# Narrow causal heads in two layers: compact q and k projections moved to their rows by DMA, four heads at a time in two slots of four banks, division after the last unit

## The reference, cut to what matters

```python
# layer 0
q, k, v = split(x @ w_attn.T + b_attn)             # 16 heads of width 16
scores = einsum('bhqd,bhkd->bhqk', q, k) * 0.25
probs = softmax(where(causal, scores, -inf))
ctx = einsum('bhqk,bhkd->bhqd', probs, v)
out = ctx @ w_proj.T + b_proj
# layer 6
A1 = causal_sdpa(q1, k1, v)                        # 16 heads, q and k of width 8, v of width 16
A2 = causal_sdpa(q2, k2, v)
diff = A1 - lam * A2
diff = (1 - lambda_init) * diff / sqrt(mean(diff * diff) + eps)   # the mean over each head's 16
out = diff @ Wproj
```

## Time and profile before

| | us |
|---|---|
| median of 3 runs | 2824.78 (2816.72 to 2827.63) |
| the profiled execution, its own time | 2828.42 |
| its span in the profile | 2826.4 |
| layer 0, from its first matmul to its last transposes | 15.24 to 182.99 |
| layer 6, from its first matmul to the end of its first output projections | 915.69 to 1236.25 |
| PE busy over the span | 2196.2 |

### The profile page before, as it was taken

One profiled execution on the slowest core, in us unless ns is written; L12 is line 12 of the kernel. 1 busy time (PEld: TensorE's weight loads), 2 busy tenths in 40 slices (PEclk: granted clock), 3 DMA queues, 4 the chain that ended last, 5 costly groups with the idle time before them and its releaser, 6 DMA issues.

```text
span 2826.4 us, 27498 instructions
## 1 busy us (share of the span) xinstructions
PE 2196.2 (78%) x9562; PEld 1357.6 (48%) x9562; DVE 1632.0 (58%) x2575; ACT 808.5 (29%) x2012; POOL 569.8 (20%) x325
## 2 busy tenths in 40 slices
PE   7885659656635989978888886444599999999986
PEld 4551224422213546656666663333466675555743
DVE  3248974869978451145555518999656614444214
ACT  1233320323312112335555401111155503444010
POOL 0121530014510002223333204566300000000010
PEclk9566878657857985569999998777699999999966
DMA  2000002010010000000000110000000100000000
GB/s 69 1 31 0 0 0 50 4 47 0 0 37 7 31 1 1 1 12 12 13 11 11 47 68 0 0 0 0 0 10 11 43 1 19 9 9 23 0 30 15
DMA packets 22031, 44.37 MB, mean 16 GB/s; under 512 B 4358, under 2 KB 16932, under 8 KB 20397
## 3 DMA queue, kind: packets, MB, share of 16 engines
q1 hardware_dynamic: 21948, 43.26, 4.7%
HBM read 42.20 MB, written 1.05 MB: 15 GB/s over the span
## 4 chain that ended last, share of the span: by engine, by line
PE 58%; DVE 33%; ACT 3%; issue 3%; POOL 1%; DMA 1%; SPq 0%; DVEq 0%; ACTq 0%; POOLq 0%
DVE big L797 7%; PE banks L1118 7%; PE banks L1087 7%; PE banks L1127 6%; PE banks L1056 6%; DVE big L1798 5%; PE banks L421 5%; PE banks L1110 3%; PE banks L372 3%; DVE big L1794 3%; PE banks L433 2%; PE banks L1352 2%; PE banks L393 2%; DVE big L792 1%; DVE big L778 1%
## 5 line engine op out<-in xcount | busy, mean ns | idle before, releaser
L1193 DVE COPY arena<-banks 128x512 f32<-128x512 f32 x196 | 135.6, 692 | 329.7 <-PE banks L1110 327.9
L218 POOL TENSOR_TENSOR ln_rstd<-ln_var_eps,neg_half 128x2 f32<-128x2 f32 x48 | 36.7, 766 | 1063.0 <-DVE ln_var_eps L206 1063.0
L1087 PE MATMUL banks<-big 128*128 128x256 f32 x784 | 235.6, 413 | 6.0 <-ACT big L1229 4.4
L1118 PE MATMUL banks<-arena,big 128*128 128x256 f32 x784 | 227.6, 414 | 6.3 <-DVE arena L1193 6.3
L1250 ACT ACTIVATE arena<-banks,arena 128x256 f32<-128x256 f32 x392 | 193.0, 499 | 62.2 <-DVE arena L1167 43.0
L709 PE MATMUL banks<-big,ident 128*128 128x512 f32 x288 | 176.8, 771 | 36.1 <-POOL big L870 36.1
L797 DVE TENSOR_TENSOR_SCAN big<-big 128x2048 f32<-128x2048 f32 x32 | 203.3, 6355 | 1.1
L870 POOL TENSOR_TENSOR big<-big 128x2048 f32<-128x2048 f32 x32 | 144.8, 4524 | 251.6 <-DVE big L797 251.6
L1127 PE MATMUL banks<-arena,big 128*128 128x256 f32 x784 | 177.0, 386 | 1.9 <-ACT big L1268 1.9
L1056 PE MATMUL banks<-x_feat,arena 128*128 128x512 f32 x392 | 176.2, 592 | 0.0
L1268 ACT ACTIVATE big<-banks 128x256 f32 (+1 forms) x196 | 75.1, 383 | 348.8 <-PE banks L1118 348.8
(11 more groups left out here) (313 smaller groups left out, 3815.4 us busy)
## 6 DMA issues: line engine op xcount, KB each, us to landing
arena<-in_L0f_w SPq DMA_DIRECT2D x1, 2048.0 KB, 8.0
arena<-in_L1a_wo SPq DMA_DIRECT2D x1, 2048.0 KB
arena<-in_L1f_gv SPq DMA_DIRECT2D x1, 2048.0 KB
arena<-in_L2a_qk_w SPq DMA_DIRECT2D x1, 2048.0 KB
arena<-in_L2x_wo SPq DMA_DIRECT2D x1, 2048.0 KB
arena<-in_L2x_q_w SPq DMA_DIRECT2D x16, 128.0 KB, 2.0
arena<-in_L2x_kv_w SPq DMA_DIRECT2D x16, 128.0 KB, 2.0
arena<-in_L2f_up SPq DMA_DIRECT2D x1, 2048.0 KB
```

Source lines behind the costliest of these rows:

```text
L1087: last = mm(ps[:, h * SEQ:(h + 1) * SEQ], q[:, b * SEQ + h * P:b * SEQ + (h + 1) * P], k[:, b * SEQ:(b + 1) * SEQ], start=True, stop=not s ...
L1118: last = mm(slot, self.v[:, 2 * b + kc, :], self.probs_t[:, u % 2, kc, :], start=(kc == 0), stop=(kc == 1))
```

## The change

Nothing outside SmallHeads changes, but for the size of a set of semaphores (32 for 26). Inside it:

- q and k weights are squeezed on DVE from 32 columns a head to 16 or 8 (eight copies into compact_w), so that eight heads of width 16, or sixteen of width 8, share one projection. There are two blocks, each with q and k and two halves of the tokens: 16 matmuls (32 records) in either layer. ACT copies them to stage. They now come before V.
- SP moves each head's rows from stage to the strip where its scores want them: 32 DMAs of 16 rows in layer 0, 64 DMAs of 8 rows in layer 6, 4 KB a row. Four more DMAs at the layer's start put a row of ones beside k. In layer 0 the bias of q and k now comes in 16 small loads instead of one.
- The first pass has nothing but masks and scores on PE, in two slots of four banks. Maxima of a group come out as 32 columns, one transpose turns them, ACT copies 32 rows, and four DMAs put them beside q. SP's loads of the next layer now stand behind all of these.
- The second pass takes four heads in one score_t, in two slots of four banks. Its exponentials and masks are in two halves as before. sum_up writes to the free last 128 columns of the slot's first two banks, in three steps of 128 columns instead of two of 256 and 128. DVE only copies the sums. The slot is free for score_t again when they are copied (sum_read).
- Turning and division come after the last unit, eight transposes and two DVE instructions a group.
- Layer 6's difference, square, mean, root and quotient go in four parts of 512 columns; the squares are made on ACT; the transposes wait for one part each.
- POOL adds the output bias of layer 0 (L592) before the masks instead of after.

```diff
-        self.qk_b = a.take(groups, 2)
-        self.row_one = a.take(1)
-        self.inv = a.take(4, 8)
-        self.probs_t = a.take(self.SLOTS, 2, 4 * P)
+        self.probs_t = a.take(2, 4, 4 * P)
+        self.compact_w = self.probs_t.rearrange("p u j t -> p (u j t)")[:, 0:8 * P].rearrange("p (k s c f) -> p k s c f", k=2, s=2, c=CH)
+        self.inv = a.take(2, 32)
...
+        self.stage = big.take(2, 2, TOKENS)
+        self.out_first = big.take(TOKENS)
+        self.max_cols = big.take(2, 4, TILES)
+        self.max_rows = big.take(groups, P, parts=32)
+        self.att = k_words[:, 0:TILES * 64 * groups].rearrange("p (t d) -> p t d", t=TILES)
+        self.att_t = q_words[:, (groups - 2) * TOKENS:groups * TOKENS].rearrange("p (c t) -> p c t", c=CH)
...
+            for g in range(self.groups):
+                blk, at = divmod(g, self.per_block)
+                for j in range(4):
+                    row = (4 * at + j) * w
+                    loads += [(self.qk_b[row:row + w, blk, :], d[n + "_qk_b"][32 * j:32 * j + w, g, :])]
...
+        e.wait_x_feat(sp, l)
+        sp.wait_ge(e.consts_made, 1)
+        for j in range(4):
+            row = 32 * j + w
+            sp.dma_start(self.k[row:row + 1].rearrange("o g t -> o (g t)"), e.ones[0:TILES * self.groups, :]).then_inc(self.rows_moved, 16)
+        for blk in range(2):
+            for s in range(2):
+                sp.wait_ge(self.staged, 4 * blk + 2 * s + 2)
+                for at in range(self.per_block):
+                    for j in range(4):
+                        row = (4 * at + j) * w
+                        dst = (self.k if s else self.q)[32 * j:32 * j + w, blk * self.per_block + at, :]
+                        sp.dma_start(dst, self.stage[row:row + w, s, blk, :]).then_inc(self.moved[blk], 16)
+        for g in range(self.groups):
+            sp.wait_ge(self.max_read, g + 1)
+            for j in range(4):
+                row = 32 * j + w
...
+        for blk in range(2):
+            for s in range(2):
+                for half in range(2):
+                    bank = B[4 * (1 - blk) + 2 * s + half]
+                    for c in range(CH):
+                        last = mm(bank, self.compact_w[:, blk, s, c, :], e.x_feat[:, c, half * BANK:(half + 1) * BANK], start=(c == 0), stop=(c == CH - 1))
+                    last.then_inc(self.proj_psum, 1)
+        pe.wait_ge(self.staged, 4)
         for t in range(TILES):
             for c in range(CH):
-                last = mm(e.y_bank(t), e.x_feat[:, c, t * P:(t + 1) * P], self.v_w[:, c, :], start=(c == 0), stop=(c == CH - 1))
+                last = mm(B[4 + t // 2][:, (t % 2) * D:(t % 2 + 1) * D], e.x_feat[:, c, t * P:(t + 1) * P], self.v_w[:, c, :], start=(c == 0), stop=(c == CH - 1))
             if t % 2:
                 last.then_inc(self.v_psum, 1)
 
-        order = self.pieces()
...
+        def score(u):
+            g, b = divmod(u, 4)
+            slot = 4 * (u % 2)
+            if u < 2:
+                pe.wait_ge(*((self.v_ready, 4) if u else (self.staged, 8)))
             else:
-                pe.wait_ge(self.maxed, u)
-            pe.wait_ge(self.proj_read, 4 * g + 3 + b // 2)
+                pe.wait_ge(self.maxed, u - 1)
+            if b == 0 and g % self.per_block == 0:
+                pe.wait_ge(self.moved[g // self.per_block], 16 * 8 * self.per_block)
+            if b == 1 and g:
+                pe.wait_ge(self.max_read, g)
             for j in range(4):
-                mask(B[j], e.ident_bf[:], causal)
+                blocks = B[slot + j][:, 0:3 * P].rearrange("p (a b) -> p a b", b=P)
+                mm(blocks[:, 0:3:2, :], e.ident_bf[:], bcast(e.causal_bf[:, P:2 * P], 1, 2), start=True, stop=False, skip_group_check=True)
...
+        def turn_max(g):
+            pe.wait_ge(self.maxed, 4 * g + 4)
+            nc.tensor.transpose(B[4][0:32, 3 * P:4 * P], self.max_cols[:, g % 2].rearrange("p j t -> p (j t)"), e.ident[:]).then_inc(self.max_psum, 1)
+
+        for u in range(self.units):
+            score(u)
+            if u % 4 == 0 and u:
+                turn_max(u // 4 - 1)
+        turn_max(G - 1)
+
+        def score_t(u):
             g, b = divmod(u, 4)
-            slot = 2 * (i % self.SLOTS)
-            if i == 0:
-                pe.wait_ge(self.maxed, 4 * G)
-                pe.wait_ge(self.proj_read, 4 * G)
-                pe.wait_ge(self.max_read, 2 * G)
-            if i >= self.SLOTS:
-                pe.wait_ge(self.exped, i - self.SLOTS + 1)
+            slot = 4 * (u % 2)
+            if u == 0:
+                pe.wait_ge(self.rows_moved, 16 * 4 * (G + 1))
+            if u >= 2:
+                pe.wait_ge(self.exped, 2 * (u - 2) + 2)
+                pe.wait_ge(self.sum_read, u - 1)
             for kc in range(2):
-                for r in range(2):
-                    rows = self.rows(2 * p + r)
-                    last = mm(B[slot + r][:, kc * SEQ:kc * SEQ + (2 - kc) * P], self.k[rows, g, b * SEQ + kc * P:b * SEQ + (kc + 1) * P],
+                for j in range(4):
+                    rows = self.rows(j, 1)
+                    last = mm(B[slot + j][:, kc * SEQ:kc * SEQ + (2 - kc) * P], self.k[rows, g, b * SEQ + kc * P:b * SEQ + (kc + 1) * P],
                               self.q[rows, g, b * SEQ + kc * P:(b + 1) * SEQ], start=True, stop=True, skip_group_check=True)
             last.then_inc(self.scored_t, 1)
         def sum_up(u):
             g, b = divmod(u, 4)
+            slot = 4 * (u % 2)
             pe.wait_ge(self.masked, 2 * u + 2)
-            for kc in range(2):
+            for half, kc, first in ((0, 0, True), (1, 0, True), (1, 1, False)):
                 for j in range(4):
+                    at = kc * SEQ + (half - kc) * P
+                    last = mm(B[slot + half][32 * j:32 * j + 32, 3 * P:4 * P], self.v[:, 2 * b + kc, 4 * (g % 4) + j, :],
+                              self.probs_t[:, u % 2, j, at:at + P], start=first, stop=(half == kc), skip_group_check=True)
             last.then_inc(self.summed, 1)
...
         score_t(0)
-        score_t(1)
-        for u in range(4 * G):
-            if u + 1 < 4 * G:
-                score_t(2 * u + 2)
+        for u in range(self.units):
+            if u + 1 < self.units:
+                score_t(u + 1)
             sum_up(u)
-            if u + 1 < 4 * G:
-                score_t(2 * u + 3)
-            if u:
-                turn_out(u - 1)
-        turn_out(4 * G - 1)
-
-        pe.wait_ge(*((self.att_ready, 1) if self.diff else (self.out_read, 4 * G)))
+
+        pe.wait_ge(self.sum_read, self.units)
+        for g in range(G):
+            if g >= 4:
+                pe.wait_ge(self.normed, g - 3)
+            for t in range(TILES):
+                last = nc.tensor.transpose(B[2 * (g % 4) + t // 4][:, (t % 4) * P:(t % 4 + 1) * P], self.out_t(g)[:, t * P:(t + 1) * P], e.ident[:])
+            last.then_inc(self.turned, 1)
         for pair in range(4):
+            pe.wait_ge(*((self.att_ready, pair + 1) if self.diff else (self.normed, G)))
...
+        for blk in range(2):
+            for s in range(2):
+                for c in range(CH):
+                    heads = self.qk_w[:, blk * self.per_block:(blk + 1) * self.per_block, s, c, :].rearrange("p g (j f) -> p g j f", f=32)
+                    ch.mark(nc.vector.tensor_copy(self.compact_w[:, blk, s, c, :].rearrange("p (g j f) -> p g j f", g=self.per_block, j=4), heads[:, :, :, 0:self.width]))
+        ch.join(dve)
+        dve.sem_inc(self.prepared, 1)
...
+            nc.vector.tensor_copy(self.out_t(g)[:, b * SEQ:(b + 1) * SEQ].rearrange("p (h t) -> p h t", h=2),
+                                  e.banks[:, slot:slot + 2, 3 * P:4 * P]).then_inc(self.sum_read, 1)
+
+        for g in range(G):
+            dve.wait_ge(self.turned, g + 1)
+            tok = e.banks[:, 2 * (g % 4):2 * (g % 4) + 2, :].rearrange("p k (t d) -> p (k t) d", d=32)
+            inv = self.inv[:, g % 2, :]
+            ch.link(dve, nc.vector.reciprocal(inv, tok[:, :, 16]))
+            nc.vector.tensor_tensor(self.att[:, :, g * 64:(g + 1) * 64].rearrange("p t (j d) -> p t j d", d=16),
+                                    tok[:, :, 0:16].rearrange("p (t j) d -> p t j d", j=4),
+                                    bcast(inv.rearrange("p (t j) -> p t j", j=4), 3, 16), ALU.mult).then_inc(self.normed, 1)
...
+            for pair in range(4):
+                ts = slice(2 * pair, 2 * pair + 2)
+                nc.vector.scalar_tensor_tensor(d[:, ts, :], self.att[:, ts, D:2 * D], self.lam, self.att[:, ts, 0:D], ALU.mult, ALU.add).then_inc(self.diffed, 1)
+            for pair in range(4):
+                heads = slice(32 * pair, 32 * pair + 32)
+                dve.wait_ge(self.squared, pair + 1)
+                ch.link(dve, nc.vector.tensor_reduce(self.ms[:, heads], self.sq[:, heads, :], AX.X, ALU.add))
+                nc.vector.tensor_scalar(self.ms[:, heads], self.ms[:, heads], 1 / 16, EPS, ALU.mult, ALU.add).then_inc(self.msq, 1)
```

(75 more changed lines are left out.)

138 lines of the change are left out of this document (30 added, 108 removed).

## The result

The changed kernel takes 2749.45 us (median of 4 runs, 2746.3 to 2755.65) against 2824.61: 0.9741 of the time before, 95% interval 0.9714 to 0.9767. The forecast was 2754. The profiled execution took 2746.3, with a span of 2744.5. One execution of the kernel before, in a later set, was slow (3281.55 at a granted clock of 0.625) and enters no comparison.

A forecast was written before the change was run, and what follows sets the result against it. PE's own work was taken to bound both layers, at the low clock in the second pass. Layer 0's -18.5 and layer 6's -52.4 made -70.9 from 2828.4, 2757.5; less 3.6 for the median, 2754; range 2700 to 2800.

The forecast's parts named there:

- layer 0: PE begins: Layer 0's start: 15 more bias loads at 0.48 and eight squeezing copies delay PE to 18.2, +3.0 us.
- layer 6: begin to first masks: Layer 6's start: 32 moves at 0.48 must land first, so the first score starts 24 us in.
- first pass, unit at half clock: First pass, masks and scores only: PE bounds a unit at 1.04 + 1.64 = 2.68, taken as 2.70 us.
- between the passes: New PE wait before the second pass: last reductions, transpose and copy, four issues, a landing; 6.6 us a layer.
- second pass, scores / sums / copy: Second-pass unit: four-head scores 1.65, sums 1.6, wait for DVE's copy 0.55; 3.8 us against 5.22.
- last copy, turning, division: After the last unit: copy 0.55, transposes 6.1 (layer 0) or 10.8 (layer 6), division adding 1.0 once.
- layer 6: difference to first y: Layer 6's end in four parts: 11.5 us to three pairs' projections done, against 17.0; gain 5.5.
- rival of dear sums: Second pass: sums cost by the record, 2.16 a unit instead of 1.6; 2781 to 2800 us; chance 0.16.
- partial overlap: Second pass: two slots overlap only in part, unit 5.2, 2816 us, no change; chance 0.06.
- Break-even near 1.5: SP's queue: spacing per small move, near 1.5 us, at which the change would gain nothing.
- slower rival: SP becomes the bound: each small move holds the queue 2.0 us instead of 0.48; 2900 us; chance 0.06.
- first rival: First pass keeps the full clock in both layers: unit 1.95 us, 38 less, 2716 us; chance 0.19.

The follow-up runs named there:

- e2: Changed kernel with a unit's second-pass scores issued only after the previous unit's sums, so the two slots never overlap: 2830.0 us.
- e6: Changed kernel with ten extra unused 128x128 bf16 matmuls behind each unit's sums in the second pass: 2702.6 us.
- e3: Changed kernel with POOL's sum of x and output bias in layer 0 waiting until the squeezed weights are made: 2736.1 us.
- e4: Changed kernel with SP moving rows group by group, first scores waiting only for the first group's eight moves: 2738.2 us.
- e12: Changed kernel run once more, unaltered, to see what differs between two profiles of one kernel: 2736.5 us.

## Why the prediction was right, point by point

| step | forecast | measured |
|---|---|---|
| layer 0: PE begins | 18.2 | 24.27 |
| layer 0: projection and V | 22.5 | 23.8 |
| layer 6: begin to first masks | 24 | 30.1 |
| first pass, unit at half clock | 2.70 | 2.56 |
| first pass, layer 0 / layer 6 | 45.8 / 91.6 | 38.9 / 87.8 |
| between the passes | 6.6 | 6.4 |
| second pass, scores / sums / copy | 1.65 / 1.6 / 0.55 | 1.66 / 1.48 / 0.60 |
| second pass, layer 0 / layer 6 | 61.3 / 122.1 | 60.3 / 120.1 |
| last copy, turning, division | 7.65 / 12.35 | 6.7 / 10.9 |
| layer 6: difference to first y | 11.5 | 13.5 |
| layer 0 / layer 6 in all | -18.5 / -52.4 | -21.0 / -51.7 |

**Right in mechanism and size:** the second pass. Four heads on four strips cost what two did, sums in 24 records cost 1.48 against 1.44, the copy is the new wait, and the clock stays at 0.50, with PE busy 84.7 of 102.0 us. e2 shows that the slots' overlap carries it, e6 that the clock is what is left of it. The rival of dear sums is refuted by 1.48, partial overlap by 3.74. With turning, the forecast had this part 15.7 and 34.0 shorter than before; it is 17.6 and 37.3 shorter, three quarters of the 72.7. One reason I gave for cheap sums does not hold: I set 0.87 for 16 records of scores, at the full clock, against 0.09 a record at the half clock, where the same records take 1.64, 0.10 each. The 1.48 is the first figure for such sums.

**Mis-sized, and cancelling.** Three terms were too small. Layer 0's start is 6.1 late: the last small load landed 2.0 later than I took from a 128 KB row, and 4.3 is DVE's instruction beside POOL (e3). I listed POOL's bias sum among the changes and gave it no price: it was moved beside DVE's first work. SP's spacing was taken as 0.48 from loads; moves from SBUF to SBUF come 0.667 apart, so 32 of them put the first score of layer 6 at 30.1 instead of 24. Break-even near 1.5 was far, so the slower rival did not decide, but its mechanism was there in small (e4): a move holds the queue for its issue, 0.667, and not for its landing, 2.3. Layer 6's end gained 3.5, not 5.5. Its last quarter was ready when I said, 9.9 after the difference began:

```profile
1150.02 0.69 DVE L528 SCALAR_TENSOR_TENSOR big<-big,arena 128x512 f32<-128x512 f32 x1
```

But I had the first projections done under the last transposes, and PE's program has all sixteen transposes first, which end at 1151.88; the first projections' 2.46 come behind them, at the half clock. Against these, the first pass was 6.9 and 3.8 shorter than forecast. Its unit at the half clock is 0.96 + 1.59, 2.56 from one to the next: 1.04 and 1.64 of the earlier trace rows are masks behind a wait and scores with nothing behind them, and the chain shows 1.01 and 1.64 again in just those places. And layer 0 ran its first units at the full clock. Errors of 6 at the start of either layer stood against errors of 4 to 7 the other way; that the totals agree within 3 is partly luck.

**The first rival** (first pass at the full clock, 0.19) is true of layer 0 in some executions (e3, e12) and false of layer 6 in all: the longest that its first pass held 1.00 was 6 us, in e4. I took it as one question for both. It is worth 10.5 in layer 0 (e12 against the profiled run).

**The remaining 9.2** between the profiles lies in layers without a change, and the forecast had nothing for it.

## What to carry to other kernels

When two passes are separated by PSUM space, count whether the slower engine's part fits under the other's in two slots: here taking out either of two such overlaps cost over 80 us, more than the whole change gained. Price moves by the issuing queue's spacing, with the row of the same kind of move if there is one, and let the first consumer wait for its own share alone. When TensorE is busy through a stretch at the low clock, ask what the stretch would take at the high one. A few unused matmuls in its gaps can cost less than the clock they bring gives back: ten a unit took 0.66 and made the unit 1.37 shorter (e6).

## What the runs showed of the hardware

- A DVE instruction on 128x2 elements took 4.48 beside a POOL sum of 128x2048 that began at the same time, ended with it, and took 0.17 when the sum came later (e3). The Trainium skill (SBUF — State Buffer, "Who interferes with whom") has only the port pair shared by VectorE and GpSimd contending, as an exclusive lock; the trace agrees, with 4.3 us of waiting for 0.17 of work.
- SP issues SBUF-to-SBUF moves of 32 and 64 KB every 0.667 us, and they land 2.3 after their issue (median, changed kernel); moves of one row of 4 KB every 0.68, the last landing after 1.77. The sixteen small bias loads of layer 0 come every 0.46, and the last lands after 4.17.
- TensorE's clock stayed at 0.50 through 130 us of second pass before, with PE busy all of them, and through 102 us of it in the changed kernel. It went to 1.00 with ten 128x128 matmuls a unit, up to 19 us after the first of them (e6). In one execution layer 0's first pass held 1.00 to its end, in another of the same kernel it fell after five units.
- A unit's sums took 1.48 as 24 records of 128 columns, and 1.44 as 16 records of 256 and 128 columns, 3072 columns in all either way: the columns decide, not the records.
